# Causal attention stage: sign of the maxima on GpSimd, multiplications merged to five, masks behind a buffer's products, shift matmul moved

## The chip, the cores and the metric

One Trainium2 chip, one of its cores. The metric is the device time of one launch in microseconds. Before the change it is 1862.38 us, the median of three runs (1860.15 to 1867.64). Lower is better.

## What is computed

Two transformer layers on x of shape (4, 1024, 128) in fp32, each with a residual and a layer norm ahead of each part:

```python
x = x + _L0_attn_ref(_layernorm(x), ...)   # causal, 16 heads of 8, relative position bias
x = x + _L0_ffn_ref(_layernorm(x), ...)
x = x + _L1_attn_ref(_layernorm(x), ...)   # 16 heads
x = x + _L1_ffn_ref(_layernorm(x), ...)

# the attention that the change touches (b = 4, n = 1024, h = 16, hd = 8)
sim = jnp.einsum('bhid,bhjd->bhij', q, k)
sim = sim + jnp.transpose(bias, (2, 0, 1)) * SCALE        # bias = rel_emb[rp_bucket]
sim = sim + causal                                        # -inf where key > query
attn = jax.nn.softmax(sim, axis=-1)
out = jnp.einsum('bhij,bhjd->bhid', attn, v)
```

## The kernel before

The program runs in phases, one after the other. The change touches one of them, `attend_causal` (tag heads1). It goes through 64 pairs of head and batch; below each pair is called a head, n. All loads and stores of a head are issued by SyncE, and the engines are tied together by semaphores. Each engine works through a list written out by hand.

What happens for a head n:

- **Loads.** q and k lie in DRAM as three bf16 parts each. `load_parts` (L463) brings six pairs of parts (48 rows) into each half of the 128 partitions of qS and kS, so that a product can run in either half of the TensorE array. The loads run four heads ahead.
- **Maxima.** `maxima(n, i)` computes the scores of whole query blocks into one of two PSUM buffers psM of 1024 columns (two banks). A buffer holds one block or two: `MAXIMA = [(7,), (0, 6), (1, 5), (2, 4), (3,)]`. Bank 0 is written from the array's half of partitions 0 to 63, bank 1 from the other. The products are at L684. Behind a block's last product come two mask matmuls (`mask`, L662) that lower what lies above the diagonal. VectorE takes the maximum of each block (L582), eight reductions a head, and then writes the negated maxima as two bf16 parts: L592 (high) and L594 (the rest), which raises `nm_ready`. In TensorE's list the maxima of head n+2 are spread over head n.
- **Shift rows.** `rows(n + 1)` (L698) transposes the 16 rows of negated maxima with one matmul of 128 columns. It waits for `nm_ready`. ScalarE copies the result to mrow (L631), and SyncE writes it by two DMAs (L469) as two more rows below the q parts, so that the scores come out with the maximum already subtracted. The first scores of head n+1 wait for that.
- **Scores and exponentials.** Nine units of 512 columns (keys down, queries across, only blocks at or below the diagonal) go through a ring of three PSUM banks. The units alternate between the array's halves. TensorE writes a unit (`scores`, L712, with masks L662 on the diagonal blocks), ScalarE takes the exponential into probs (L651). The shift rows use a slot of the same ring between units 3 and 4, so `scores` of a unit waits until ScalarE has taken the unit three slots before.
- **Bias near the diagonal.** GpSimd multiplies the first 256 columns (128 for the last key block) of each key block by exp of the bias (L619), eight multiplications a head in the order `NEAR_ORDER`, each as soon as the unit named in `NEAR_AFTER` has been taken. Then it stages v of the next head (L610).
- **Values.** `values(n - 1, part)` multiplies probs and v in fp32 (L734 for both query blocks of a pair, L738 for one). A query pair c sits in its own quarter of the array's columns. The 26 entries of `VALUES` (query pair, key block) are dealt out over three parts in the list of the next head. Each matmul in fp32 is two instructions in the trace. Part 0 waits for all eight multiplications of head n-1 (`near_done`). ScalarE copies the result (L637), SyncE stores it (L473).

TensorE's list for head n, which sets the order of everything:

```python
scores(n, 0); scores(n, 1); maxima(n + 2, 0); maxima(n + 2, 1)
scores(n, 2); scores(n, 3)
values(n - 1, 0)
rows(n + 1)
scores(n, 4); maxima(n + 2, 2); scores(n, 5); scores(n, 6); maxima(n + 2, 3)
values(n - 1, 1)
scores(n, 7); scores(n, 8); maxima(n + 2, 4)
values(n - 1, 2)
```

The phase `attend_full` (heads3) does the same for the second attention, without masks, and there GpSimd already writes the two parts of the negated maxima (L871, L873) from reductions that negate (L852).

Of the kernel before, what the change touches and what calls it, by code (L numbers as in the profile page):

```python
# [18 lines left out]
ALU = mybir.AluOpType  # L19
ACT = mybir.ActivationFunctionType  # L20
AXX = mybir.AxisListType.X
# [3 lines left out]
P = 128  # L25
B = 4
# [449 lines left out]
def attend_causal(nc, m, g):  # L476
# [7 lines left out]
    ORDER = [0, 1, 2, 3, ROWS, 4, 5, 6, 7, 8]  # L484
    MAXIMA = [(7,), (0, 6), (1, 5), (2, 4), (3,)]
    NM = len(MAXIMA)
    NEAR_ORDER = [0, 1, 7, 2, 6, 3, 5, 4]
    NEAR_AFTER = [0, 2, 3, 4, 5, 6, 7, 8]
    VALUES = [[(0, 0), (1, 0), (2, 0), (3, 0), (0, 1), (1, 1), (2, 1), (3, 1), (0, 2), (1, 2), (2, 3), (3, 4), (0, 3)],
              [(0, 4), (1, 3), (2, 2), (3, 2), (0, 5), (1, 4)],  # L490
              [(0, 6), (1, 5), (2, 4), (3, 3), (0, 7), (1, 6), (2, 5)]]

    ENDS = VALUES[2][-4:]

    def place(kb, qb):

# [8 lines left out]
    def near_width(kb):  # L505
        return min(NEAR, T - kb * P)
# [24 lines left out]
    with nc.Block() as block:  # L531
# [36 lines left out]
        @block.vector  # L568
        def _(dve):
            for u in range(BUFS):  # L570
                dve.memset(kS[u][:, :], 1.0).then_inc(cleared, 1)
            for n in range(NG):
                p = n % 2
                for i, blocks in enumerate(MAXIMA):
                    dve.wait_ge(maxima_done, n * NM + i + 1)
                    at = 0
                    for qb in blocks:
                        if i == 0 and n >= 2:

                            dve.wait_ge(nm_ready, n - 1)  # L580
                        w = (qb + 1) * P
                        last = dve.tensor_reduce(mx[:, p, qb:qb + 1], psM[(n * NM + i) % 2][:, at:at + w], AXX, ALU.max)  # L582
                        if qb != blocks[-1]:
                            last.then_inc(block_taken, 1)
                        at += w
                    last.then_inc(max_taken, 1)
                dve.wait_ge(max_taken, (n + 1) * NM)
                dve.wait_ge(block_taken, (n + 1) * (TPB - NM))
                if n >= 2:

                    dve.wait_ge(slot_done, ring.rows(n - 2) + 1)
                dve.tensor_scalar(nm[:, p, 0, :], mx[:, p, :], -1.0, None, ALU.mult).then_inc(nm_hi, 1)  # L592
                dve.wait_ge(nm_hi, n + 1)
                dve.scalar_tensor_tensor(nm[:, p, 1, :], mx[:, p, :], -1.0, nm[:, p, 0, :], ALU.mult, ALU.subtract).then_inc(nm_ready, 1)  # L594

        @block.gpsimd
        def _(pool):
# [7 lines left out]
            def stage_v(n):  # L605
# [3 lines left out]
                src = g["v_all"][:, :, :, :].rearrange("p h (b t) e -> p (h b) t e", b=B)[:, n, :, :]  # L609
                pool.tensor_copy(v_ones[n % 3][:, :, 0:HD], src).then_inc(v_staged, 1)  # L610

            stage_v(0)
            for n in range(NG):
                pr = probs[n % 2]
                for kb, unit in zip(NEAR_ORDER, NEAR_AFTER):
                    pool.wait_ge(slot_taken, ring.index(n, unit) + 1)
                    a, w = place(kb, kb), near_width(kb)
                    eb = g["ebias"][:, n // B, :]
                    pool.tensor_tensor(pr[:, a:a + w], pr[:, a:a + w], bass.AP(eb.tensor, eb.offset + NEAR - 1, [list(eb.ap[0]), [-1, w]]),  # L619
                                       ALU.mult).then_inc(near_done, 1)  # L620
                if n + 1 < NG:
                    stage_v(n + 1)

# [34 lines left out]
        def _(pe):  # L658
# [6 lines left out]
            def maxima(n, i):  # L665

                if n >= NG:
                    return
                u, k = n % BUFS, n * NM + i
                if k >= 2:  # L670

                    pe.wait_ge(max_taken, k - 1)
                if i == 0:
                    pe.wait_ge(s_loaded[u], (n // BUFS + 1) * 64)
                ps = psM[k % 2]
                at = 0
                for qb in MAXIMA[i]:
                    w = (qb + 1) * P
                    for bank in range(2):
                        a, z = max(at, bank * CH), min(at + w, (bank + 1) * CH)  # L680
                        if a >= z:
                            continue
                        r, ends = HALF * bank, z == at + w
                        last = pe.matmul(ps[:, a:z], qS[u][r:r + PROWS, qb * P:(qb + 1) * P], kS[u][r:r + PROWS, a - at:z - at], start=True, stop=not ends)  # L684
                        if ends:
                            last = mask(ps[:, z - P:z], r, 1)
                    at += w
                last.then_inc(maxima_done, 1)

            def rows(n):  # L690
# [28 lines left out]
            def values(n, part):  # L719
# [2 lines left out]
                    return  # L722
                if part == 0:
                    pe.wait_ge(v_staged, n + 1)
                    pe.wait_ge(near_done, (n + 1) * TPB)
                    if n > 0:
                        pe.wait_ge(o_taken, n)
                pr, v = probs[n % 2][:, :], v_ones[n % 3]
                for c, kb in VALUES[part]:
                    out = psO[c * VW:(c + 1) * VW, 0:2 * P]  # L730
# [17 lines left out]
            for n in range(NG):  # L748
# [3 lines left out]
                maxima(n + 2, 1)  # L752
                scores(n, 2)
                scores(n, 3)
                values(n - 1, 0)
                rows(n + 1)
                scores(n, 4)
                maxima(n + 2, 2)
                scores(n, 5)
# [1245 lines left out]
```

## Time and profile before

| | us |
|---|---|
| median of three runs | 1862.38 |
| lowest, highest | 1860.15, 1867.64 |
| the profiled execution's own time | 1864.79 |
| its span, first to last instruction | 1863.1 |
| mean granted TensorE clock | 0.933 of 2.4 GHz |

Busy time of the engines over the whole span, and the same in 40 slices of 46.6 us (each digit is a tenth; the stage of the change fills slices 3 to 10 and most of the 11th):

```profile
PE 1636.9 (88%) x19058; PEld 1045.2 (56%) x19082; DVE 1517.5 (81%) x2250; ACT 1255.1 (67%) x2481; POOL 773.8 (42%) x1489
PE   5499999999745999999999639999999999999835
...
DVE  7599999999444999988555769999999999999354
```

PE is TensorE's matmuls, PEld its weight loads, DVE is VectorE, ACT ScalarE, POOL GpSimd, SP SyncE. A row of the groups below reads: line, engine, operation, output and inputs, shapes, count, then busy time and mean duration, then the idle time of the engine before them and what ended it. A row of the timeline reads: start, length, engine, line, operation; several instructions of one form that follow or overlap each other are drawn together with their count, and the bracket is the idle time before them. The ends of matmuls are modelled, their starts are recorded.

### The profile page before, as it was taken

To read this page: it belongs to the slowest core of one execution; us is meant where nothing else is said; L and a number is where in the kernel's file an instruction comes from. 1 tells how busy PE (TensorE), PEld (TensorE's weight loads), DVE (VectorE), ACT (ScalarE), POOL (GpSimd) and SP (SyncE) were. 2 spreads that over 40 slices of the span, in tenths; PEclk is the share of its full clock that TensorE was granted. 3 is DMA by queue.
4 is the path that set the end of the run, shared out by engine and by line. 5 is a ranking of instruction groups with operands and counts; after the bars stand their busy time and mean duration, and the time that the engine had idled before them with its cause. 6 is when DMAs were issued, how large, how long until landed. Compare 5 with 4: busy or idle time off the path is not lost. (4 is left out here: it accounts for less than half of the span.)

```text
span 1863.1 us, 48171 instructions
## 1 busy us (share of the span) xinstructions
PE 1636.9 (88%) x19058; PEld 1045.2 (56%) x19082; DVE 1517.5 (81%) x2250; ACT 1255.1 (67%) x2481; POOL 773.8 (42%) x1489
## 2 busy tenths in 40 slices
PE   5499999999745999999999639999999999999835
PEld 3266766776544887877677413444444444444424
DVE  7599999999444999988555769999999999999354
ACT  7378888888623444454333627988988988988734
POOL 4388888888635001000000123444444444444345
PEclk9599999999865999999999867999999999999967
DMA  8422222222171755573000351111111111111041
GB/s 270 161 77 87 86 84 87 86 85 84 44 157 26 103 93 89 94 90 59 1 1 0 122 188 40 56 58 53 55 59 54 54 59 54 54 59 48 20 102 46
DMA packets 132965, 141.87 MB, mean 76 GB/s; under 512 B 22989, under 2 KB 106122, under 8 KB 132746
## 3 DMA queue, kind: packets, MB, share of 16 engines
q1 hardware_dynamic: 132314, 138.79, 29.3%
q8 instruction: 148, 2.42, 0.5%
q14 instruction: 71, 0.58, 0.1%
q10 hardware_dynamic: 432, 0.07, 0.0%
HBM read 92.70 MB, written 44.98 MB: 74 GB/s over the span
## 5 line engine op out<-in xcount | busy, mean ns | idle before, releaser
L852 DVE TENSOR_REDUCE heads_mx<-heads_psM 128x1 f32<-128x1024 f32 x512 | 602.3, 1220 | 37.8 <-PE heads_psM L941 21.8
L921 ACT ACTIVATE heads_probs<-heads_psS 128x512 f32<-128x512 f32 x1024 | 546.0, 601 | 76.6 <-PE heads_psS L964 70.6
L890 POOL TENSOR_TENSOR heads_masked<-heads_probs,g_tri 128x128 f32<-128x128 f32 x512 | 233.7, 456 | 359.6 <-ACT heads_probs L921 359.5
L619 POOL TENSOR_TENSOR heads_probs<-heads_probs,one_ebias 128x256 f32<-128x256 f32 (+1 forms) x512 | 341.6, 690 | 82.1 <-ACT heads_probs L651 81.6
L651 ACT ACTIVATE heads_probs<-heads_psS 128x512 f32<-128x512 f32 x576 | 316.4, 603 | 65.9 <-PE heads_psS L662 60.7
L582 DVE TENSOR_REDUCE heads_mx<-heads_psM 128x1 f32<-128x1024 f32 (+7 forms) x512 | 349.6, 750 | 10.7 <-PE heads_psM L662 9.7
L941 PE MATMUL heads_psM<-heads_kS,heads_qS 48*128 48x512 bf16 x1024 | 229.9, 394 | 27.7 <-DMA heads_kS<-k_parts 18.8
L964 PE MATMUL heads_psS<-heads_qS,heads_kS 50*128 50x512 bf16 x1024 | 237.5, 388 | 0.7 <-ACT heads_probs L921 0.3
L1486 ACT ACTIVATE trees_hid_hi<-trees_hid 128x512 fp32r<-128x512 f32 x192 | 121.7, 634 | 153.3 <-DVE trees_hid L1507 151.8
L1507 DVE SCALAR_TENSOR_TENSOR trees_hid<-trees_psH,g_b,trees_chosen 128x512 f32<-128x512 f32 x192 | 144.0, 750 | 32.5 <-DMA trees_chosen<-leaf_choice 14.7
L684 PE MATMUL heads_psM<-heads_kS,heads_qS 48*128 48x512 bf16 (+3 forms) x768 | 147.8, 335 | 22.1 <-DMA heads_kS<-k_parts 19.2
L989 PE MATMUL heads_psO<-heads_probs,heads_ones_only 128*32 128x128 f32 x1920 | 161.8, 283 | 0.0
L990 PE MATMUL heads_psO<-heads_probs,heads_v_ones 128*32 128x128 f32 x1920 | 155.7, 273 | 0.0
L734 PE MATMUL heads_psO<-heads_probs,heads_v_ones 128*32 128x256 f32 x1280 | 150.9, 396 | 2.3 <-POOL heads_probs L619 2.0
L983 PE MATMUL heads_psO<-heads_probs,heads_ones_only 128*32 128x256 f32 x1280 | 148.7, 390 | 0.0
L712 PE MATMUL heads_psS<-heads_qS,heads_kS 50*128 50x512 bf16 (+3 forms) x768 | 141.4, 334 | 7.3 <-DMA heads_qS<-heads_mrow 5.4
L738 PE MATMUL heads_psO<-heads_probs,heads_v_ones 128*32 128x128 f32 x2048 | 136.6, 279 | 0.0
L1514 DVE SCALAR_TENSOR_TENSOR trees_hid_lo<-trees_hid,trees_hid_hi 128x512 fp32r<-128x512 f32 x192 | 134.2, 699 | 0.1
L964 PEld LDWEIGHTS heads_psS<-heads_qS,heads_kS 50*128 50x128 bf16 x1024 | 69.5, 93 | 114.3 <-ACT heads_probs L921 55.0
L1600 POOL COPY wide_qs<-two_qkT 128x1024 f32 (+1 forms) x4 | 4.2, 1039 | 282.6 <-SPq L1544 179.6
L983 PE MATMUL heads_psO<-heads_probs,heads_v_ones 128*32 128x256 f32 x768 | 120.9, 394 | 0.0
L989 PEld LDWEIGHTS heads_psO<-heads_probs,heads_ones_only 128*32 128x32 f32 x1920 | 72.5, 108 | 81.9 <-issue 81.8
(248 smaller groups left out, 3125.0 us busy)
## 6 DMA issues: line engine op xcount, KB each, us to landing
heads_qS<-q_parts SPq DMA_DIRECT2D x256, 96.0 KB
heads_kS<-k_parts SPq DMA_DIRECT2D x256, 96.0 KB
trees_chosen<-leaf_choice SPq DMA_DIRECT2D x96, 256.0 KB
head_outputs<-heads_oT SPq DMA_DIRECT2D x128, 128.0 KB
heads_qS<-heads_mrow SPq DMA_DIRECT2D x256, 4.0 KB
q_parts<-open_parts SPq DMA_DIRECT2D x8, 384.0 KB, 3.7
k_parts<-open_parts SPq DMA_DIRECT2D x8, 384.0 KB, 4.9
q_parts<-proj_parts SPq DMA_DIRECT2D x8, 384.0 KB, 3.3
```

Source lines behind the costliest of these rows:

```text
L582: last = dve.tensor_reduce(mx[:, p, qb:qb + 1], psM[(n * NM + i) % 2][:, at:at + w], AXX, ALU.max)
L619: pool.tensor_tensor(pr[:, a:a + w], pr[:, a:a + w], bass.AP(eb.tensor, eb.offset + NEAR - 1, [list(eb.ap[0]), [-1, w]]), ALU.mult).then_i ...
L651: act.activation(probs[n % 2][:, slot * CH:(slot + 1) * CH], ring.bank(i)[:, :], ACT.Exp).then_inc(slot_taken, 1)
L734: last = pe.matmul(out.rearrange("p (q w) -> p q w", w=P), v[:, kb, :], bass.AP(pr.tensor, a, [list(pr.ap[0]), [far - a, 2], [1, P]]), sta ...
L852: dve.tensor_reduce(mx[:, n % 2, k:k + 1], psM[k % 2][:, :], AXX, ALU.max, negate=True).then_inc(max_taken, 1)
L890: pool.tensor_tensor(masked[n % 2][:, kb, :], probs[n % 2][:, kb, kb * P:(kb + 1) * P], g["tri"][:, 0:P], ALU.mult).then_inc(near_done, 1)
L921: act.activation(probs[n % 2][:, kb, h * CH:(h + 1) * CH], ring.bank(i)[:, :], ACT.Exp).then_inc(slot_taken, 1)
L941: last = pe.matmul(psM[k % 2][:, h * CH:(h + 1) * CH], qS[u][r:r + PROWS, k * P:(k + 1) * P], kS[u][r:r + PROWS, h * CH:(h + 1) * CH], sta ...
L964: pe.matmul(ring.bank(i)[:, :], kS[u][r:r + RROWS, kb * P:(kb + 1) * P], qS[u][r:r + RROWS, h * CH:(h + 1) * CH], start=True, stop=True).t ...
L983: pe.matmul(out.rearrange("p (q w) -> p q w", w=P), v_ones[v][:, kb, :] if kb < c else ones_only[:, :], both, start=kb == 0, stop=False, t ...
L989: pe.matmul(out[:, 0:P], ones_only[:, :], pr[:, c, :], start=False, stop=False, tile_position=(0, c * VW))
L990: pe.matmul(out[:, P:2 * P], v_ones[v][:, kb, :], pr[:, b, :], start=False, stop=False, tile_position=(0, c * VW))
```

## The change

- **VectorE** no longer writes the negated maxima. Its reductions negate their result.
- **GpSimd** writes them (`minus_maxima`): a copy to bf16 and a subtraction, for head n+1, ahead of the multiplications of head n and behind the staging of v.
- **The multiplications** become five: key blocks (0, 1) after unit 2, 7 after unit 3, 6 after unit 5, (2, 3) after unit 6, (5, 4) after unit 8. A pair is one instruction over two blocks of 256 columns.
- **Values** are dealt out as 9, 10 and 7 entries instead of 13, 6 and 7. Part 0 waits for four of the five multiplications of its head, part 1 for all.
- **Maxima**: the products of a buffer alternate between its two banks, and all masks of the buffer come behind them.
- **The shift matmul** `rows(n + 1)` comes ahead of `values(n - 1, 0)` instead of behind it.

```diff
-    NEAR_ORDER = [0, 1, 7, 2, 6, 3, 5, 4]
-    NEAR_AFTER = [0, 2, 3, 4, 5, 6, 7, 8]
-    VALUES = [[(0, 0), (1, 0), (2, 0), (3, 0), (0, 1), (1, 1), (2, 1), (3, 1), (0, 2), (1, 2), (2, 3), (3, 4), (0, 3)],
-              [(0, 4), (1, 3), (2, 2), (3, 2), (0, 5), (1, 4)],
-              [(0, 6), (1, 5), (2, 4), (3, 3), (0, 7), (1, 6), (2, 5)]]
+    NEARS = [((0, 1), 2), ((7,), 3), ((6,), 5), ((2, 3), 6), ((5, 4), 8)]
+    NEAR_FIRST = 4
+    VALUES = [[(0, 0), (1, 0), (2, 0), (3, 0), (0, 1), (1, 1), (2, 1), (3, 1), (0, 2)],
+              [(1, 2), (2, 2), (3, 2), (0, 3), (1, 3), (2, 3), (3, 4), (0, 4), (1, 4), (0, 5)],
+              [(2, 4), (3, 3), (0, 6), (1, 5), (2, 5), (0, 7), (1, 6)]]
...
-                        last = dve.tensor_reduce(mx[:, p, qb:qb + 1], psM[(n * NM + i) % 2][:, at:at + w], AXX, ALU.max)
+                        last = dve.tensor_reduce(mx[:, p, qb:qb + 1], psM[(n * NM + i) % 2][:, at:at + w], AXX, ALU.max, negate=True)
...
-                dve.tensor_scalar(nm[:, p, 0, :], mx[:, p, :], -1.0, None, ALU.mult).then_inc(nm_hi, 1)
-                dve.wait_ge(nm_hi, n + 1)
-                dve.scalar_tensor_tensor(nm[:, p, 1, :], mx[:, p, :], -1.0, nm[:, p, 0, :], ALU.mult, ALU.subtract).then_inc(nm_ready, 1)
...
+            def minus_maxima(n):
+
+                p = n % 2
+                pool.wait_ge(max_taken, (n + 1) * NM)
+                pool.wait_ge(block_taken, (n + 1) * (TPB - NM))
+                if n >= 2:
+                    pool.wait_ge(slot_done, ring.rows(n - 2) + 1)
+                pool.tensor_copy(nm[:, p, 0, :], mx[:, p, :]).then_inc(nm_hi, 1)
+                pool.wait_ge(nm_hi, n + 1)
+                pool.tensor_tensor(nm[:, p, 1, :], mx[:, p, :], nm[:, p, 0, :], ALU.subtract).then_inc(nm_ready, 1)
+
+            def weight(n, blocks):
+
+                pr, eb, w = probs[n % 2][:, :], g["ebias"][:, n // B, :], near_width(blocks[0])
+                a = place(blocks[0], blocks[0])
+                step = place(blocks[-1], blocks[-1]) - a
+                at = bass.AP(pr.tensor, a, [list(pr.ap[0]), [step, len(blocks)], [1, w]])
+                by = bass.AP(eb.tensor, eb.offset + NEAR - 1, [list(eb.ap[0]), [0, len(blocks)], [-1, w]])
+                pool.tensor_tensor(at, at, by, ALU.mult).then_inc(near_done, 1)
+
             stage_v(0)
+            minus_maxima(0)
             for n in range(NG):
-                pr = probs[n % 2]
-                for kb, unit in zip(NEAR_ORDER, NEAR_AFTER):
+                if n + 1 < NG:
+                    minus_maxima(n + 1)
+                for blocks, unit in NEARS:
                     pool.wait_ge(slot_taken, ring.index(n, unit) + 1)
-                    a, w = place(kb, kb), near_width(kb)
-                    eb = g["ebias"][:, n // B, :]
-                    pool.tensor_tensor(pr[:, a:a + w], pr[:, a:a + w], bass.AP(eb.tensor, eb.offset + NEAR - 1, [list(eb.ap[0]), [-1, w]]),
-                                       ALU.mult).then_inc(near_done, 1)
+                    weight(n, blocks)
                 if n + 1 < NG:
                     stage_v(n + 1)
...
+                for j in range(max(len(of) for of in runs)):
+                    for bank in range(2):
+                        if j < len(runs[bank]):
+                            qb, a, z, first = runs[bank][j]
+                            r = HALF * bank
+                            pe.matmul(ps[:, a:z], qS[u][r:r + PROWS, qb * P:(qb + 1) * P], kS[u][r:r + PROWS, first:first + z - a],
+                                      start=j == 0, stop=j + 1 == len(runs[bank]) and (bank + 1) * CH not in [-(-e // CH) * CH for e in ends])
+                for s in range(2):
+                    for z in ends:
+                        r = HALF * ((z - 1) // CH)
+                        later = [e for e in ends if z < e <= -(-z // CH) * CH]
+                        last = pe.matmul(ps[:, z - P:z], g["masks"][r:r + HALF, s, 0, :], g["masks"][r:r + HALF, s, 1, :], start=False,
+                                         stop=s == 1 and not later)
...
-                    pe.wait_ge(near_done, (n + 1) * TPB)
+                    pe.wait_ge(near_done, n * len(NEARS) + NEAR_FIRST)
                     if n > 0:
                         pe.wait_ge(o_taken, n)
+                if part == 1:
+                    pe.wait_ge(near_done, (n + 1) * len(NEARS))
...
                 scores(n, 3)
+                rows(n + 1)
                 values(n - 1, 0)
-                rows(n + 1)
                 scores(n, 4)
```

## Rows read from the trace of the kernel before

**Rows 1.** Busy time by stretch: us, engines (instructions), clock, DMA.

```profile
100.00:440.00 340.00, 334.69 (x5783) 237.55 (x5780) 331.30 (x531) 284.95 (x583) 290.90 (x478) 1.00 0.28 86
```

**Rows 2.** Groups by shape, GpSimd's multiplications, 100 to 440 us.

```profile
L619 POOL TENSOR_TENSOR heads_probs<-heads_probs,one_ebias 128x256 f32<-128x256 f32 x372 | 261.8, 724 | 49.1 <-ACT heads_probs L651 48.6
L619 POOL TENSOR_TENSOR heads_probs<-heads_probs,one_ebias 128x128 f32<-128x128 f32 x53 | 23.9, 451 | 0.0
```

**Rows 3.** Timeline of VectorE over one head: start, length.

```profile
260.62 0.70 DVE L592 TENSOR_SCALAR heads_nm<-heads_mx 128x8 bf16<-128x8 f32 x1
261.35 0.17 DVE L594 SCALAR_TENSOR_TENSOR heads_nm<-heads_mx,heads_nm 128x8 bf16<-128x8 f32 x1
261.44 5.42 DVE L582 TENSOR_REDUCE heads_mx<-heads_psM 128x1 f32<-128x1024 f32 x8
266.90 0.69 DVE L592 TENSOR_SCALAR heads_nm<-heads_mx 128x8 bf16<-128x8 f32 x1
```

**Rows 4.** Line L592 over the whole span: duration minimum/median/maximum in ns.

```profile
L592 DVE TENSOR_SCALAR heads_nm<-heads_mx x64: 171/694/707, 78.4 to 484.9; 128x8 bf16<-128x8 f32 x64
```

**Rows 5.** Timeline of GpSimd over the same head.

```profile
258.51 2.78 POOL L619 TENSOR_TENSOR heads_probs<-heads_probs,one_ebias 128x256 f32<-128x256 f32 x4
261.24 0.23 POOL L610 COPY heads_v_ones<-one_v_all 128x64 f32<-128x64 f32 x1
261.43 0.73 POOL L619 TENSOR_TENSOR heads_probs<-heads_probs,one_ebias 128x256 f32<-128x256 f32 x1
...
264.09 3.47 POOL L619 TENSOR_TENSOR heads_probs<-heads_probs,one_ebias 128x256 f32<-128x256 f32 x5 [0.49 <-ACT heads_probs L651]
```

**Rows 6.** Timeline of TensorE's matmuls where one head ends.

```profile
266.06 0.29 PE L738 MATMUL heads_psO<-heads_probs,heads_v_ones 128*32 128x128 f32 x3
266.32 0.40 PE L712 MATMUL heads_psS<-heads_qS,heads_kS 50*128 50x512 bf16 x2
```

**Rows 7.** Waits, 100 to 440 us: total us, times, longest.

```profile
PEld heads_psS L712 <- ACT heads_probs L651: 19.7, 106, 0.2
PEld heads_psS L712 <- DMA heads_qS<-heads_mrow: 13.9, 35, 1.0
```

**Rows 8.** Groups by shape, the third stage's reductions, 1100 to 1780 us.

```profile
L852 DVE TENSOR_REDUCE heads_mx<-heads_psM 128x1 f32<-128x1024 f32 x512 | 602.3, 1220 | 37.8 <-PE heads_psM L941 21.8
```

**Rows 9.** Timeline of GpSimd in the third stage: the sign pair.

```profile
1304.82 0.19 POOL L871 CAST heads_nm<-heads_mx 128x8 bf16<-128x8 f32 x1
1305.09 0.20 POOL L873 TENSOR_TENSOR heads_nm<-heads_mx,heads_nm 128x8 bf16<-128x8 f32 x1
```

**Rows 10.** Timeline of ScalarE: units 7 and 8, units 4 to 6, units 7 and 8.

```profile
259.19 1.08 ACT L651 ACTIVATE heads_probs<-heads_psS 128x512 f32<-128x512 f32 x2 [0.29 <-PE heads_psS L662]
...
263.42 1.77 ACT L651 ACTIVATE heads_probs<-heads_psS 128x512 f32<-128x512 f32 x3 [0.16 <-PE heads_psS L662]
265.47 1.08 ACT L651 ACTIVATE heads_probs<-heads_psS 128x512 f32<-128x512 f32 x2 [0.29 <-PE heads_psS L662]
```

**Rows 11.** Timeline of TensorE: values part 0, shift matmul, scores of unit 4.

```profile
261.62 0.64 PE L734 MATMUL heads_psO<-heads_probs,heads_v_ones 128*32 128x256 f32 x8
...
262.40 0.51 PE L738 MATMUL heads_psO<-heads_probs,heads_v_ones 128*32 128x128 f32 x9
262.73 0.22 PE L698 MATMUL heads_psS<-g_identb,heads_nm 128*16 128x128 bf16 x1
262.88 0.39 PE L712 MATMUL heads_psS<-heads_qS,heads_kS 50*128 50x512 bf16 x1
```

**Rows 12.** Timeline of TensorE: maxima of blocks (2, 4), values part 1, scores.

```profile
263.92 0.40 PE L684 MATMUL heads_psM<-heads_kS,heads_qS 48*128 48x384 bf16 x2
264.09 0.29 PE L662 MATMUL heads_psM<-g_masks 64*128 64x128 bf16 x3
...
264.36 0.30 PE L738 MATMUL heads_psO<-heads_probs,heads_v_ones 128*32 128x128 f32 x2
...
264.93 0.40 PE L712 MATMUL heads_psS<-heads_qS,heads_kS 50*128 50x128 bf16 x3
```

More of the change, by code:

```diff
@@ L486, in attend_causal @@
     NM = len(MAXIMA)
-    NEAR_ORDER = [0, 1, 7, 2, 6, 3, 5, 4]
-    NEAR_AFTER = [0, 2, 3, 4, 5, 6, 7, 8]
-    VALUES = [[(0, 0), (1, 0), (2, 0), (3, 0), (0, 1), (1, 1), (2, 1), (3, 1), (0, 2), (1, 2), (2, 3), (3, 4), (0, 3)],
-              [(0, 4), (1, 3), (2, 2), (3, 2), (0, 5), (1, 4)],
-              [(0, 6), (1, 5), (2, 4), (3, 3), (0, 7), (1, 6), (2, 5)]]
-    ENDS = VALUES[2][-4:]
+    NEARS = [((0, 1), 2), ((7,), 3), ((6,), 5), ((2, 3), 6), ((5, 4), 8)]
[3 more added lines that the diff above has]
+              [(2, 4), (3, 3), (0, 6), (1, 5), (2, 5), (0, 7), (1, 6)]]
+    ENDS = [(3, 3), (2, 5), (0, 7), (1, 6)]
     def place(kb, qb):
@@ L586, in _ @@
                     last.then_inc(max_taken, 1)
[L587 to L591, printed above, removed]
-                dve.tensor_scalar(nm[:, p, 0, :], mx[:, p, :], -1.0, None, ALU.mult).then_inc(nm_hi, 1)
-                dve.wait_ge(nm_hi, n + 1)
-                dve.scalar_tensor_tensor(nm[:, p, 1, :], mx[:, p, :], -1.0, nm[:, p, 0, :], ALU.mult, ALU.subtract).then_inc(nm_ready, 1)
         @block.gpsimd
@@ L675, in maxima @@
                 ps = psM[k % 2]
-                at = 0
+                runs, ends, at = ([], []), [], 0
                 for qb in MAXIMA[i]:
@@ L680, in maxima @@
                         a, z = max(at, bank * CH), min(at + w, (bank + 1) * CH)
[L681 to L686, printed above, removed]
-                    at += w
+                        if a < z:
+                            runs[bank].append((qb, a, z, a - at))
+                    at += w
+                    ends.append(at)
+                for j in range(max(len(of) for of in runs)):
[11 more added lines that the diff above has]
+                                         stop=s == 1 and not later)
                 last.then_inc(maxima_done, 1)
```

## The prediction

> **What bounds the kernel now.** I read the busy time by stage first. The diff touches only the causal attention stage, so every other stage should stay as it is. Between 100 and 440 us, all inside that stage, the clock is at its full level (2.4 GHz), and TensorE (335 of 340 us) and VectorE (331 of 340) both look full [rows 1]. Instructions that come once a head stand there 53 times [rows 2], so a head takes 340 / 53 = 6.415 us.
>
> Two engines are seldom both the limit, so next I looked at what fills VectorE's head. Its eight reductions run without a gap, 5.42 us. Then comes L592, 8 elements in 0.70 us, and L594, 8 elements in 0.17 us [rows 3]. An operation on 8 elements doesn't need 0.7 us: over the 64 heads L592's minimum is 171 ns, its median 694 [rows 4]. GpSimd's line gives the reason: L592 starts at 260.62 and ends at 261.32, and GpSimd's multiplication beside it is the last of four that end at 258.51 + 2.78 = 261.29 [rows 3, 5]. So L592 waits for GpSimd. About 0.5 us of each head is a wait that is booked as VectorE's work; its own is near 5.42 + 0.17 + 0.17 and gaps, 5.8 us. It is not the limit.
>
> TensorE is. A smooth head takes 266.90 - 260.62 = 6.28 us [rows 3], and at its end the values products (until 266.06 + 0.29 = 266.35) and the next head's first scores (266.32) follow without idle time [rows 6]. Its waits in the stretch are two: unit 3's scores for the exponential of unit 0 (19.7 us over 106 waits), and in some heads the first scores for the DMA of the shift rows (13.9 us over 35 waits, up to 1.0) [rows 7]. The second makes most of the difference between 6.28 and the mean of 6.415.
>
> **The change, part by part.**
>
> *VectorE loses L592 and L594*, 0.70 + 0.17 us of its line. Since it isn't the limit, I book nothing. Reductions with the sign inside cost the same: the third stage has them at 1220 ns for 1024 elements [rows 8], and the 4608 elements of a head's eight take 5.42 us here, 1.20 for 1024 [rows 3].
>
> *GpSimd gains the sign pair.* The third stage has the same pair: L871 starts at 1304.82, L873 0.27 us later and lasts 0.20 [rows 9].
>
> *Eight multiplications become five* over the same elements. 128 elements take 451 ns, 256 take 724: 273 ns for each further 128, about 178 fixed [rows 2]. Back to back the 256-wide ones follow each other every (3.47 - 0.72) / 4 = 0.69 us [rows 5]. A 512-wide one is in no row; worked out, it holds GpSimd for 0.69 + 2 x 0.273 = 1.23 us. Bounds: above 1.37, two single ones; below 1.0, if the two-block pattern hid more than one start. I take 1.23. Three merges save about 3 x 0.14 = 0.4 us a head of an engine with idle time: nothing booked. But the last group, blocks 5 and 4, is now one piece of 1.23 us that can only start when unit 8's exponential is done; today block 5 is multiplied before that.
>
> *The shift matmul (L698) moves ahead of the first values part.* This step decides. It waits for nm_ready, and behind it in TensorE's order stand values part 0 and the scores of unit 4, so ScalarE's exponentials from unit 4 on wait too, and SyncE's issue of the shift rows and of the loads behind it hangs on the copy of its result. When is nm ready? GpSimd's order is: last group of head n-1, staging of v, sign pair of head n+1, groups of head n. Counted from the end of unit 8's exponential, 259.19 + 1.08 = 260.27 [rows 10]:
> - to GpSimd's start 0.07 to 0.08 (the exponential of unit 4 ends at 263.42 + 0.60 = 264.02, GpSimd starts at 264.09 [rows 5, 10])
> - last group 1.23
> - staging of v to the next instruction 0.19 (261.24 to 261.43 [rows 5])
> - sign pair 0.27 + 0.20 [rows 9]
> - to TensorE 0.07, taken from the hand-over above.
>
> That is 2.04 us, so L698 starts at 260.27 + 2.04 = 262.31. TensorE is ready for it where values part 0 starts today, at 261.62 [rows 11]. So TensorE stands still for 0.69 us in every head. Today nm is ready at 261.35 + 0.17 = 261.52 [rows 3], L698 comes at 262.73, and nothing is lost.
>
> What is late next follows round the loop. *From L698 to values part 0*: 0.05 if nothing drains between them (bounds 0 and 0.15). Today L698 starts 0.18 us before the modelled end of the values ahead of it (262.40 + 0.51 = 262.91), while the scores behind it start 0.15 after it, though it streams only 128 columns [rows 11]. I read that as no drain between values and L698, and one before scores. The Trainium skill, "TensorEngine Tiling (Array Packing)", Key Properties, says that changing the tiling mode drains TensorE and another tile of the same mode doesn't. If by that page L698 is a mode of its own, a head costs 0.1 us more, 6 us in all; the row speaks for the mode of the values. *Values part 0*: today's part 1 has 256 columns for each quarter of the array and takes 264.36 to 264.93 = 0.57 [rows 12]. Today's part 0 has 640 and takes 262.73 - 261.62 = 1.11 up to L698. The 0.10 of changing to scores apart, 128 columns cost (1.11 - 0.47) / 3 = 0.21. The new part 0 has 512: 0.57 + 2 x 0.21 = 1.00. *From unit 4's scores* (262.88) to the end of unit 8's exponential (265.47 + 1.08 = 266.55) it is 3.67 today, plus 0.21 because part 1 grows by 128 columns: 3.88 [rows 10, 11]. Round the loop: 2.04 + 0.05 + 1.00 + 3.88 = **6.97 us a head**, against 6.415.
>
> In that loop VectorE (5.42 and gaps) and GpSimd (3 x 1.23 + 0.69 + 0.41 + 0.19 + 0.47 = 5.45) have room. The shift rows' DMA gets 0.69 us more of it than in a smooth head, where its longest wait is 1.0 and most are far shorter [rows 7], so nearly all of these waits vanish; that is in the difference already, which is taken against the mean.
>
> *Maxima products alternate between the halves, masks behind them.* That gains only if a mask of one half holds back the product of the other. In block pair (2, 4) the 384-column product of one half and the 512-column product of the other start together at 263.92 (two instructions within 0.40 us), and masks start at 264.09, though two of them stand ahead of the 512-column product in the program [rows 12]. The halves already overlap: nothing booked, bounds -0.05 and +0.05 us for the two pair buffers that lie inside the loop.
>
> The sum: 61 heads in the steady state x (6.97 - 6.415) = 33.9 us. The start adds about 0.5 (head 1's L698 already waits behind head 0's last group), and the end gives back about 0.7, as values part 0 of the last head waits for four groups instead of all. So 1864.8 + 33.7 for the profiled execution, whose time is 2.4 above the median of 1862.4; against the median **1896 us**. A group of 1.37 with a drain and the buffers' 0.05 (+0.29 a head) gives 1914, a group of 1.0 with the buffers' -0.05 (-0.28 a head) 1879.
>
> **Rivals.**
> *Faster: VectorE is the limit after all.* It has no gap in a smooth head [rows 3]. If so, and if nm came in time, a head would fall to TensorE's own work, 6.28 less part of the 19.7 / 53 = 0.37 us that unit 3 waits [rows 7], about 6.1: 61 x -0.3 = -19, so 1843. It decides if nm is ready within 261.62 - 260.27 = 1.35 us of unit 8's exponential, which leaves 0.54 for the 512-wide group. A 128-wide block alone takes 0.45, and the wait inside L592 speaks against it as well.
>
> *Same: masks do hold back the other half today, or the group is much shorter.* If TensorE kept to strict order, each pair buffer inside the loop would now wait out its masks, and the change would take some 0.2 us off each of the two: 6.97 - 0.40 = 6.57, 61 x 0.155 = +9, so 1872. The pair (2, 4) row speaks against it [rows 12]. The Trainium skill, "TensorE: Matmul & The Clock Gate", Part 3, says that matmuls start strictly in program order; this trace doesn't agree, it shows the product 0.17 us ahead of earlier masks. A group of 0.85 us would give the same 1872.
>
> *Same: the change doesn't do what it says*, and the sign pair is taken ahead of the last group, so that nobody waits. The order of the loop excludes it. It would leave 6.3 to 6.415 us a head, 1856 to 1862.
>
> **How the numbers follow.** Slower by the wait of L698, 1896 (own range 1877 to 1914): 0.77. The cases near today's time, 1856 to 1872: 0.13. The faster one, 1843: 0.10. The range leaves out the faster case and part of the middle one: 1864 to 1914. A measurement of this kernel tells about 0.5%, 9 us, from no change.
>
> **What would show it.** TensorE idle for about 0.7 us before L698 in each head, put down to GpSimd; L698 2.0 us behind unit 8's exponential; GpSimd's 512-wide form at about 1.27 us; even distances of 6.97 us between heads; hardly a wait for the DMA of the shift rows; VectorE's share of the stage down from 0.97 to about 0.8 without any gain. Wrong would be: no idle time ahead of L698, a 512-wide form under 0.9 us, or a head under 6.4 us.

## The result, and the profile after

The changed kernel takes **1894.64 us** (median of four runs, 1893.71 to 1896.67) against 1862.64 for the kernel before on the same chip: a ratio of 1.0169, 95% interval 1.0148 to 1.0190. It is 32.0 us slower; 1896 was predicted, within 1864 to 1914. Its profiled execution took 1894.83, with a span of 1893.1. Below, the stretch from 100 to 440 us as in [rows 1], then GpSimd's 512-wide piece by shape as in [rows 2] (total, mean ns, idle time before them and what ended it), then the waits as in [rows 7].

```profile
100.00:440.00 340.00, 312.14 (x5343) 214.37 (x5341) 269.55 (x393) 249.73 (x540) 265.75 (x393) 1.00 0.26 79
```

```profile
L622 POOL TENSOR_TENSOR heads_probs<-heads_probs,one_ebias 128x512 f32<-128x512 f32 x148 | 188.3, 1272 | 25.9 <-ACT heads_probs L662 25.9
```

```profile
ACT heads_probs L662 <- PE heads_psS L673: 90.3, 147, 0.9
DVE heads_mx L582 <- PE heads_psM L707: 70.9, 99, 1.0
PE heads_psS L719 <- POOL heads_nm L613: 27.9, 49, 0.6
```

Once-a-head work stands here 49 times, not 53: 340 / 49 = 6.94 us a head. VectorE is down from 331 us to 270 of the 340, GpSimd from 291 to 266, and TensorE too, from 335 to 312. Nobody is full any more, which is the mark of a loop of waits. The wait that closes it is new: in every head the matmul at L719 (the shift matmul, L698 before) stands 27.9 / 49 = 0.57 us for GpSimd's pair. The waits for the shift rows' DMA, 13.9 us in [rows 7], are gone from the list.

One head of it by time. GpSimd: last group, staging of v, sign pair, next head's first two groups, and the last group of the head after:

```profile
265.76 1.27 POOL L622 TENSOR_TENSOR heads_probs<-heads_probs,one_ebias 128x512 f32<-128x512 f32 x1 [0.26 <-ACT heads_probs L662]
266.97 0.24 POOL L602 COPY heads_v_ones<-one_v_all 128x64 f32<-128x64 f32 x1
267.14 0.20 POOL L611 CAST heads_nm<-heads_mx 128x8 bf16<-128x8 f32 x1
267.42 0.20 POOL L613 TENSOR_TENSOR heads_nm<-heads_mx,heads_nm 128x8 bf16<-128x8 f32 x1
267.87 1.69 POOL L622 TENSOR_TENSOR heads_probs<-heads_probs,one_ebias 128x512 f32<-128x512 f32 x2 [0.26 <-ACT heads_probs L662]
...
272.70 1.27 POOL L622 TENSOR_TENSOR heads_probs<-heads_probs,one_ebias 128x512 f32<-128x512 f32 x1 [0.27 <-ACT heads_probs L662]
```

TensorE where the shift matmul stands:

```profile
266.83 0.27 PE L673 MATMUL heads_psS<-g_masks 64*128 64x128 bf16 x2
267.67 0.22 PE L719 MATMUL heads_psS<-g_identb,heads_nm 128*16 128x128 bf16 x1 [0.57 <-POOL heads_nm L613]
267.77 0.64 PE L757 MATMUL heads_psO<-heads_probs,heads_v_ones 128*32 128x256 f32 x8
...
268.78 0.39 PE L733 MATMUL heads_psS<-heads_qS,heads_kS 50*128 50x512 bf16 x1
```

ScalarE: units 7 and 8, unit 0, units 1 to 3, units 4 to 6, units 7 and 8, unit 0 of the next head:

```profile
264.60 1.08 ACT L662 ACTIVATE heads_probs<-heads_psS 128x512 f32<-128x512 f32 x2 [0.65 <-PE heads_psS L673]
265.95 0.60 ACT L662 ACTIVATE heads_probs<-heads_psS 128x512 f32<-128x512 f32 x1 [0.26 <-PE heads_psS L673]
...
266.70 1.58 ACT L662 ACTIVATE heads_probs<-heads_psS 128x512 f32<-128x512 f32 x3
...
269.31 1.58 ACT L662 ACTIVATE heads_probs<-heads_psS 128x512 f32<-128x512 f32 x3 [0.93 <-PE heads_psS L673]
271.54 1.09 ACT L662 ACTIVATE heads_probs<-heads_psS 128x512 f32<-128x512 f32 x2 [0.65 <-PE heads_psS L673]
272.89 0.60 ACT L662 ACTIVATE heads_probs<-heads_psS 128x512 f32<-128x512 f32 x1 [0.27 <-PE heads_psS L673]
```

The loop closes: unit 8's exponential ends at 264.60 + 1.08 = 265.68, L719 starts 1.99 later at 267.67, values part 0 0.10 later, scores 4 after another 1.01, and the next unit 8's exponential ends at 272.63, 3.85 after these. Sum 6.95. Last groups lie 272.70 - 265.76 = 6.94 apart.

Now read the same rows for something the prediction did not ask. The shift matmul writes into the ring of three banks, in slot 4, so it also waits until ScalarE has taken slot 1, unit 1. That exponential is the first of the three at 266.70 and ends near 266.70 + 0.60 = 267.30. TensorE is ready at 266.83 + 0.27 = 267.10. So two waits stand side by side, and the profile names only the one that ends last.

### The profile page after: what moved, and what is told of

It reads as the page before. It is cut to its first block and busy times, and to the rows that moved or that the text cites. A ratio compares the mean times of both kernels' runs of the same rounds, so it can differ in the third digit from the quotient of the medians.

```text
span 1893.1 us, 47979 instructions
## 1 busy us (share of the span) xinstructions
PE 1637.0 (86%) x19058; PEld 1035.6 (55%) x19082; DVE 1470.6 (78%) x2122; ACT 1238.2 (65%) x2481; POOL 770.0 (41%) x1425
## 5 line engine op out<-in xcount | busy, mean ns | idle before, releaser
L622 POOL TENSOR_TENSOR heads_probs<-heads_probs,one_ebias 128x512 f32<-128x512 f32 (+2 forms) x320 | 314.6, 1000 | 91.2 <-ACT heads_probs L662 91.1
L701 PE MATMUL heads_psM<-heads_kS,heads_qS 48*128 48x512 bf16 (+3 forms) x768 | 164.7, 332 | 22.1 <-DMA heads_kS<-k_parts 19.0
L733 PE MATMUL heads_psS<-heads_qS,heads_kS 50*128 50x512 bf16 (+3 forms) x768 | 155.9, 331 | 1.0 <-ACT heads_probs L662 0.8
L707 PE MATMUL heads_psM<-g_masks 64*128 64x128 bf16 x1024 | 125.8, 220 | 0.0
```

The costliest lines, as they stand in the source:

```text
L622: pool.tensor_tensor(at, at, by, ALU.mult).then_inc(near_done, 1)
L733: last = pe.matmul(ps[:, at:at + count], kS[u][r:r + RROWS, kb * P:(kb + 1) * P], qS[u][r:r + RROWS, first:first + count], start=True, sto ...
```

## The experiments

Kernels are compared by times since a head's first exponential, that of unit 0. In the changed kernel the shift matmul starts 267.67 - 265.95 = 1.72 after it.

**Is it the one moved line?** e1 is the changed kernel with it moved back, e2 the kernel before with it alone moved.

```diff
# e1, from the changed kernel (e2: the reverse, on the kernel before)
-                rows(n + 1)
                 values(n - 1, 0)
+                rows(n + 1)
                 scores(n, 4)
```

> The changed kernel with one part undone: the shift matmul comes behind values part 0 again. Theory (TensorE's wait for GpSimd's sign pair ahead of the shift matmul is the whole loss): the pair is ready 2.0 us behind unit 8's exponential, TensorE gets to the matmul only 1.35 + 0.90 = 2.25 us behind it, so the wait is gone and a head falls from 6.94 to between 6.28 and 6.37 us. Time 1855 to 1861 us. Rival (the new sharing out of the values, the merged multiplications or the masks behind the products cost the time): it stays between 1880 and 1895.

> The kernel before with one part of the change alone: the shift matmul ahead of values part 0, sign pair still on VectorE. Theory: VectorE has the pair ready 0.1 us before TensorE gets there, so there is no wait; time 1855 to 1862 us. Rival (the place of the matmul costs by itself, by a drain or by the exponentials behind it coming later): 1870 to 1896.

e1: 1855.39 us (1852.95 to 1858.74), inside the range of its theory; ratio to before 0.9941 (0.9924 to 0.9958). With that one line back the changed kernel is the faster one, so the line is worth 1.0169 against 0.9941, 2.3%. e2: 1888.50 (1886.55 to 1891.25), ratio 1.0124 (1.0105 to 1.0142). My theory expected e2 to be free, because VectorE's L594 is ready early enough. It is not free, and e2's TensorE, then ScalarE and VectorE beside it, say why:

```profile
271.60 0.22 PE L698 MATMUL heads_psS<-g_identb,heads_nm 128*16 128x128 bf16 x1 [0.35 <-ACT heads_probs L651]
```

```profile
270.10 0.60 ACT L651 ACTIVATE heads_probs<-heads_psS 128x512 f32<-128x512 f32 x1 [0.26 <-PE heads_psS L662]
...
270.85 1.59 ACT L651 ACTIVATE heads_probs<-heads_psS 128x512 f32<-128x512 f32 x3
```

```profile
270.90 0.17 DVE L594 SCALAR_TENSOR_TENSOR heads_nm<-heads_mx,heads_nm 128x8 bf16<-128x8 f32 x1
```

VectorE is indeed not the cause: L594 ends at 271.07, and TensorE is idle only from 271.60 - 0.35 = 271.25 on. The matmul starts 1.50 after the first exponential and 0.15 after unit 1's exponential (270.85 + 0.60 = 271.45), and the wait of 0.35 us is put down to ScalarE. That is the slot of the ring. The time lies in the range of e2's rival, that the place costs by itself; the next runs separate the two.

**Is GpSimd's order the cause, or the ring?** e3 is the changed kernel with the sign pair of head n+2 ahead of the last group, so that nm is ready long before.

```diff
             minus_maxima(0)
+            minus_maxima(1)
             for n in range(NG):
-                if n + 1 < NG:
-                    minus_maxima(n + 1)
                 for blocks, unit in NEARS:
+                    if unit == 8 and n + 2 < NG:
+                        minus_maxima(n + 2)
                     pool.wait_ge(slot_taken, ring.index(n, unit) + 1)
```

> The changed kernel with GpSimd's sign pair of head n+2 taken ahead of the last group of head n (blocks 5 and 4), instead of the pair of head n+1 behind it. Theory: the maxima are complete about when unit 8's exponential ends, the pair is ready before TensorE gets to the shift matmul, the wait of 0.69 us is gone, a head takes 6.2 to 6.35 us; time 1850 to 1861 us. Rival (GpSimd's work, not its order, holds the loop): it stays over 1885.

e3: 1883.95 us (1880.42 to 1887.63), ratio 1.0105 (1.0086 to 1.0124). The theory of the prediction, that nothing else waits once nm is in time, is wrong. In e3's code the line numbers are one higher again: L720 is the shift matmul, L663 the exponential. e3's TensorE, then its ScalarE, then its waits between 100 and 440 us:

```profile
269.73 0.22 PE L720 MATMUL heads_psS<-g_identb,heads_nm 128*16 128x128 bf16 x1 [0.35 <-ACT heads_probs L663]
269.85 0.64 PE L758 MATMUL heads_psO<-heads_probs,heads_v_ones 128*32 128x256 f32 x8
...
270.86 0.39 PE L734 MATMUL heads_psS<-heads_qS,heads_kS 50*128 50x512 bf16 x1
```

```profile
268.22 0.60 ACT L663 ACTIVATE heads_probs<-heads_psS 128x512 f32<-128x512 f32 x1 [0.26 <-PE heads_psS L674]
...
268.98 1.58 ACT L663 ACTIVATE heads_probs<-heads_psS 128x512 f32<-128x512 f32 x3
...
274.97 0.60 ACT L663 ACTIVATE heads_probs<-heads_psS 128x512 f32<-128x512 f32 x1 [0.26 <-PE heads_psS L674]
```

```profile
PE heads_psS L720 <- ACT heads_probs L663: 17.9, 51, 0.4
```

A head takes 274.97 - 268.22 = 6.75 us. GpSimd is no longer named; L720 stands 17.9 / 51 = 0.35 us for unit 1's exponential (it ends at 269.58, L720 starts at 269.73, 1.51 after the first exponential). So the late pair costs 6.94 - 6.75 = 0.19 us a head; the rest is there without it.

The rest can be split with e1, where values part 0 comes first. Its TensorE, then unit 0's exponential on ScalarE in three heads in a row:

```profile
271.99 0.64 PE L757 MATMUL heads_psO<-heads_probs,heads_v_ones 128*32 128x256 f32 x8
...
272.88 0.22 PE L719 MATMUL heads_psS<-g_identb,heads_nm 128*16 128x128 bf16 x1
```

```profile
270.90 0.60 ACT L662 ACTIVATE heads_probs<-heads_psS 128x512 f32<-128x512 f32 x1 [0.31 <-PE heads_psS L673]
...
277.14 0.60 ACT L662 ACTIVATE heads_probs<-heads_psS 128x512 f32<-128x512 f32 x1 [0.27 <-PE heads_psS L673]
...
283.39 0.60 ACT L662 ACTIVATE heads_probs<-heads_psS 128x512 f32<-128x512 f32 x1 [0.27 <-PE heads_psS L673]
```

e1's head is 283.39 - 277.14 = 6.25, a little under the 6.28 to 6.37 expected. Its values start 271.99 - 270.90 = 1.09 after the first exponential. From there it takes 0.89 to the shift matmul and 0.15 more to scores 4, as before [rows 11]. e3 takes 0.12 from the shift matmul to values and 1.01 from there. Thus e3's scores 4 come (1.51 - 1.09) + (1.13 - 1.04) = 0.42 + 0.09 = 0.51 later: 0.42 is the wait for the ring, 0.09 the order of the two. That is the 6.75 - 6.25 = 0.50 of its head. (The expectation of e9 below puts the bank's release 0.05 behind unit 1's exponential; the rows of e2 and e3 show 0.15 from that end to the start of the matmul.)

**Does the length of GpSimd's chain set the head, in the changed kernel?** e6 puts a memset of 256 columns between the staging of v and the sign pair; e5 does block 5 after unit 7 and block 4 after unit 8 as before, so only 256 columns are left behind unit 8.

```diff
# e6
                     stage_v(n + 1)
+                    pool.memset(spare[:, :], 0.0)
# e5
-    NEARS = [((0, 1), 2), ((7,), 3), ((6,), 5), ((2, 3), 6), ((5, 4), 8)]
+    NEARS = [((0, 1), 2), ((7,), 3), ((6,), 5), ((2, 3), 6), ((5,), 7), ((4,), 8)]
```

> The changed kernel with a memset of 256 columns on GpSimd between the staging of v and the sign pair, about 0.25 us of its time. Theory (in the changed kernel GpSimd's chain ends last, ring and TensorE earlier): every head grows by the same 0.25 us, to 7.19; 61 x 0.25 = +15, 1906 to 1914 us. Rival (another wait ends last): under 1900 us.

> The changed kernel with the last group split: block 5 after unit 7, block 4 after unit 8. Taken alone the chain behind unit 8's exponential would shrink by 0.54 us; but GpSimd is still at the group of blocks (2, 3) when unit 7 is done, so block 4 starts about 0.4 us later than it could, and the pair is only 0.14 us earlier. Below that stands the ring's wait, 0.19 us under today's head. Theory: 6.80 us a head, 1884 to 1889 us. Rival (the chain behind unit 8 is all that counts and there is no second wait): 6.40 us, 1862 us.

e6: 1911.64 us (1910.25 to 1911.87), ratio 1.0262 (1.0245 to 1.0280). Its GpSimd:

```profile
264.97 1.27 POOL L623 TENSOR_TENSOR heads_probs<-heads_probs,one_ebias 128x512 f32<-128x512 f32 x1 [0.26 <-ACT heads_probs L664]
...
266.35 0.31 POOL L635 MEMSET heads_spare<- 128x256 f32 x1
266.61 0.19 POOL L612 CAST heads_nm<-heads_mx 128x8 bf16<-128x8 f32 x1
...
272.17 1.27 POOL L623 TENSOR_TENSOR heads_probs<-heads_probs,one_ebias 128x512 f32<-128x512 f32 x1 [0.26 <-ACT heads_probs L664]
```

The memset holds GpSimd for 266.61 - 266.35 = 0.26 us and the head grows from 6.94 to 7.20, by the same 0.26. In that direction GpSimd's chain passes one to one into the head. e5: 1889.28 us (1888.59 to 1889.69), ratio 1.0133 (1.0115 to 1.0151), 0.3 us above its theory's range; head 6.78 by its shift matmuls:

```profile
265.07 0.22 PE L719 MATMUL heads_psS<-g_identb,heads_nm 128*16 128x128 bf16 x1 [0.41 <-POOL heads_nm L613]
271.85 0.22 PE L719 MATMUL heads_psS<-g_identb,heads_nm 128*16 128x128 bf16 x1 [0.41 <-POOL heads_nm L613]
```

The wait for GpSimd falls from 0.57 to 0.41 us. One 256-wide piece instead of the 512-wide takes 0.54 us off the chain (1.27 to 0.73), but GpSimd does its four last pieces in a row there and starts the last one late, so only 0.16 us reaches TensorE.

**Can the move be made free?** e9 is e3 with the shift matmul behind the first four entries of values part 0. TensorE then has work while unit 1's exponential ends. e10 does that to the kernel before, and e11 to the changed kernel with its late pair. The lines below are the main part of the edit; beside them, head 0 issues its shift matmul by itself, as it has no values ahead.

```diff
-                for c, kb in VALUES[part]:
+                for e, (c, kb) in enumerate(VALUES[part]):
+                    if part == 0 and e == 4 and shift is not None:
+                        rows(shift)
```

> The changed kernel with the sign pair early (as in the run before that did so) and the shift matmul after the first four of values part 0's nine entries, that is about 0.45 us further back, still ahead of most of them. The trace of the run with the early pair shows the matmul waiting for the ring: its PSUM bank is free only 0.05 us behind unit 1's exponential, which ends 1.36 us behind the head's first exponential, 0.3 to 0.4 us later than TensorE gets there. Theory (two waits stand at that place, GpSimd's and the ring's, and either alone holds TensorE): both are past at the new place, a head takes 6.24 us as with the matmul behind part 0, time 1853 to 1858 us. Rival (coming ahead of the values costs by itself, by drains or by later exponentials): over 1870 us.

> The kernel before with one edit: the shift matmul after the first four entries of values part 0, 0.45 us behind the place where it lost 24 us. The sign pair stays on VectorE, nothing else is changed. Theory (what the move costs is the ring: the bank of unit 1, whose exponential ends 1.36 us behind the head's first): no wait is left, a smooth head takes 6.28 us, and the copy of the rows comes 0.2 us earlier, so there are fewer waits for the shift rows' DMA; 1855 to 1862 us. Rival (the matmul among or ahead of the values costs by itself): 1870 us or more.

> The changed kernel with the one edit of moving the shift matmul after the first four entries of values part 0; the sign pair stays behind GpSimd's last group. There the ring is free (1.5 us behind the first exponential), but the pair is ready only at 1.72. Theory (the two waits stand side by side, each with its own time): 0.18 us of waiting for GpSimd is left, a head takes 6.42 us, 1860 to 1867 us. Rival (only one of the waits is real): 6.24 us and 1854, or 6.94 us and 1895.

e9: 1854.04 us (1853.17 to 1855.57), ratio 0.9956 (0.9940 to 0.9973). e10: 1856.29 (1855.89 to 1859.51), 0.9960 (0.9945 to 0.9975). e11: 1864.66 (1863.56 to 1867.30), 1.0004 (0.9994 to 1.0013). All three fall in the range that the two waits give. In e9 TensorE no longer stands still ahead of the matmul, and the values go on at once:

```profile
268.82 0.64 PE L761 MATMUL heads_psO<-heads_probs,heads_v_ones 128*32 128x256 f32 x8
269.28 0.22 PE L720 MATMUL heads_psS<-g_identb,heads_nm 128*16 128x128 bf16 x1
269.28 0.39 PE L761 MATMUL heads_psO<-heads_probs,heads_v_ones 128*32 128x256 f32 x3
```

e11's ScalarE has unit 0 at 261.30 and 267.73, 6.43 apart against e9's 6.24 (267.74 and 273.98): the late pair costs 0.19 here as it does from e3 to the changed kernel, and TensorE's weight load for L719 waits for GpSimd once a head, 25.4 us over 53 between 100 and 440.

e10 shows that the move can pay. Its smooth head is 6.28 us as before, but the shift rows leave earlier, and the waits for their DMA fall from 13.9 us over 35 [rows 7] to 7.3 over 23. That is 6.6 us less in 340, and an estimate of 6.6 x 61 x 6.415 / 340 = 7.6 us for the whole stage, against 1864.61 - 1856.29 = 8.3 measured on the same chip. e1, e9 and e10 are the fastest kernels of the study; the intervals of their ratios overlap, and I don't rank them.

**What is the order of the maxima worth?** e4 is the changed kernel with the maxima code of before.

```diff
-                runs, ends, at = ([], []), [], 0
...
+                at = 0
+                for qb in MAXIMA[i]:
...
+                        if ends:
+                            last = mask(ps[:, z - P:z], r, 1)
```

> The changed kernel with the maxima products and masks in their old order. Theory (the array's halves already ran beside each other before): no difference, 1892 to 1897 us. Rival (today's order gains a little inside the pair buffers): the old order costs 0.1 to 0.4 us a head more, 1901 to 1919 us.

e4: 1898.99 us (1897.12 to 1901.55), ratio 1.0181 (1.0163 to 1.0199). Its ScalarE:

```profile
260.98 0.60 ACT L662 ACTIVATE heads_probs<-heads_psS 128x512 f32<-128x512 f32 x1 [0.26 <-PE heads_psS L673]
...
264.35 1.77 ACT L662 ACTIVATE heads_probs<-heads_psS 128x512 f32<-128x512 f32 x3 [0.93 <-PE heads_psS L673]
266.62 1.09 ACT L662 ACTIVATE heads_probs<-heads_psS 128x512 f32<-128x512 f32 x2 [0.51 <-PE heads_psS L673]
267.97 0.60 ACT L662 ACTIVATE heads_probs<-heads_psS 128x512 f32<-128x512 f32 x1 [0.26 <-PE heads_psS L673]
```

The time lies between the ranges of the theory (no difference, up to 1897) and of the rival (from 1901). 6.99 a head against 6.94, so the new order gains 0.05 us. It is gained between units 4 and 7, where blocks (1, 5) and (2, 4) are: 266.62 - 264.35 = 2.27 against 271.54 - 269.31 = 2.23 in the changed kernel. The intervals of the two kernels overlap in time; the distance between heads tells them apart.

**Is VectorE really not the limit before?** e7 is the kernel before with a ninth reduction, of 256 elements, into a spare column.

```diff
+                        if qb == 1:
+                            dve.tensor_reduce(spare[:, :], psM[(n * NM + i) % 2][:, at:at + w], AXX, ALU.max)
                         last = dve.tensor_reduce(mx[:, p, qb:qb + 1], psM[(n * NM + i) % 2][:, at:at + w], AXX, ALU.max)
```

> The kernel before with a ninth reduction of 256 columns on VectorE in each head, 0.34 us back to back. Theory (half a microsecond of its head is the wait for GpSimd inside the sign's first instruction, and that wait shortens by as much): that instruction falls from 0.70 to about 0.4 us, and the time stays within 5 us of the kernel before. Rival (VectorE is the limit in a smooth head): +0.34 x 61 = +21 us.

e7: 1870.94 us (1868.26 to 1872.39), ratio 1.0044 (1.0030 to 1.0058). VectorE, then GpSimd beside it, then the waits:

```profile
259.60 0.42 DVE L584 TENSOR_REDUCE heads_spare<-heads_psM 128x1 f32<-128x256 f32 x1
...
263.04 0.37 DVE L595 TENSOR_SCALAR heads_nm<-heads_mx 128x8 bf16<-128x8 f32 x1
```

```profile
259.91 3.47 POOL L622 TENSOR_TENSOR heads_probs<-heads_probs,one_ebias 128x256 f32<-128x256 f32 x5 [0.49 <-ACT heads_probs L654]
```

```profile
PEld heads_psM L687 <- DVE heads_mx L585: 9.5, 52, 0.2
```

The sign instruction (L592 before) falls from 0.70 us [rows 3] to 0.37 and ends at 263.41, just behind GpSimd's piece (259.91 + 3.47 = 263.38), as its length being a wait demands. But the added 0.34 us isn't free: TensorE now waits in every head for VectorE to give back a buffer of psM, 9.5 / 52 = 0.18 us each time, a wait that L684 does not have before. The distance between heads grows by the same 0.18, from 6.28 to 6.46 (the exponentials of unit 0 start at 256.35 and 262.81). Neither number of the expectation came true: the price is 8.6 us against the 1862.36 of the same chip, above the 5 of my theory and far below the 21 of the rival. It is less than 61 x 0.18 = 11 because the waits for the shift rows' DMA shrink, from 13.9 us [rows 7] to 5.3. VectorE had slack, but only about 0.34 - 0.18 = 0.16 us of it at that place, not the 0.5 that the sign instruction's wait suggests.

**Can the ring's wait be covered by scores instead?** e8 moves values part 0 and the shift matmul between units 2 and 3.

```diff
-    ORDER = [0, 1, 2, 3, ROWS, 4, 5, 6, 7, 8]
+    ORDER = [0, 1, 2, ROWS, 3, 4, 5, 6, 7, 8]
...
                 scores(n, 2)
-                scores(n, 3)
-                rows(n + 1)
                 values(n - 1, 0)
+                rows(n + 1)
+                scores(n, 3)
                 scores(n, 4)
```

> The changed kernel with values part 0 between the scores of units 2 and 3 and the shift matmul behind it, ahead of unit 3; its slot in the ring is then between units 2 and 3. In the kernel before TensorE stands 0.2 us still ahead of unit 3, for unit 0's exponential. Theory (a head is as long as TensorE's list with its waits): part 0 covers that wait, the shift matmul is reached 1.75 to 1.85 us behind the first exponential, when GpSimd's pair (2.0 us behind unit 8's exponential) and the ring are just ready; a head takes 6.05 to 6.2 us, the DMA of the shift rows being what may hold it now; time 1838 to 1852 us. Rival (the order of the values is indifferent, or ScalarE runs dry): 1855 us or more.

e8: 1880.12 us (1879.25 to 1881.22), ratio 1.0097 (1.0080 to 1.0114). A clear miss. Its ScalarE, and the waits:

```profile
269.75 0.27 ACT L642 ACTIVATE heads_mrow<-heads_psS 16x128 bf16<-16x128 f32 x1 [0.32 <-PE heads_psS L719]
270.15 2.07 ACT L662 ACTIVATE heads_probs<-heads_psS 128x512 f32<-128x512 f32 x4
```

```profile
PEld heads_psS L733 <- ACT heads_probs L662: 28.5, 153, 0.2
```

Unit 3's exponential starts 2.57 us after the first (267.58) where the changed kernel has it at about 1.7, and unit 6 needs its slot. ScalarE has nothing to do behind unit 2 until the shift matmul is through. The weight loads of the scores wait for ScalarE three times a head, 28.5 / 51 = 0.56 us together, where e9 has 10.7 us over 54 waits, 0.20 a head. That is most of the difference of their heads (6.67 and 6.24); which of the three waits sets it was not separated. A bank of its own for the shift rows would take them out of the ring; it wasn't tried, since no bank was free.

## Why the prediction came out as it did

The terms of the loop, predicted and measured in the changed kernel:

| step | predicted | measured |
|---|---|---|
| unit 8's exponential to the shift matmul | 2.04 | 1.99 |
| of it the 512-wide group, to the next start | 1.23 | 1.21 |
| TensorE idle ahead of it | 0.69 | 0.57 |
| to values part 0 | 0.05 | 0.10 |
| values part 0 | 1.00 | 1.01 |
| scores 4 to the end of unit 8's exponential | 3.88 | 3.85 |
| a head | 6.97 | 6.94 |

The 512-wide group lasts 1.27 as a single instruction, but the staging of v starts 266.97 - 265.76 = 1.21 behind its start, and that is what the sum needs. The head grew by 6.94 - 6.415 = 0.525 us, times 61 heads 32.0, which is the difference of the medians.

**Right:** that the moved matmul decides and waits for GpSimd, the length of the 512-wide group inside its bounds, the price of the larger values part, that the DMA waits vanish, and that VectorE's share falls (to 269.6 / 340 = 0.79) without a gain. That three merged multiplications save nothing by themselves was not tested.

**Wrong, though the sum doesn't show it:** the step "TensorE is ready for it where values part 0 starts today", followed by GpSimd as the only thing waited for. The shift matmul is also the fifth slot of a ring of three, a wait that the code of `rows` states, and it never entered the sum. By e2 and e3 it ends at 1.51 us after the first exponential, so with nm in time the move still costs 0.42 us of waiting. Only the last 0.2 of the 0.6 us belongs to GpSimd alone. The total was right because the later of two parallel waits was the one summed, and that it was the later one had not been checked: that part is luck. Two statements built on it fall: the rival in which "nobody waits" at 6.3 to 6.415 a head (e3 measured 6.75), and the 1.35 us by which nm would have to be ready for the faster case.

**Mis-sized:** the step from the shift matmul to values, taken as 0.05, is 0.10 (0.12 in e3), inside the bounds given. The maxima order, booked at nothing with bounds of 0.05, gains 0.05 a head (e4), the whole bound; the reason given against a gain, the overlap in [rows 12], is true of the pair shown, but some time was left in it. The rival of strict order would have given 0.2 for each buffer, and that is refuted. VectorE was called far from the limit: for this change that held, yet e7 shows that 0.34 us more costs about half of it (0.18 a smooth head).

**Not asked:** the other parts together gain. With the line back e1 is at 0.9941, 9.4 us under the 1864.84 of its chip. Some 61 x (6.28 - 6.25) = 2 us of them are the smooth head, where the maxima order gains; another 3 go with less waiting for the shift rows' DMA (e1's list has 11.0 us over 37 waits against 13.9 over 35 in [rows 7], so 2.9 less in 340 us). These two make about 5 of the 6 us by which e1's profiled execution (1858.74) lies under that of before (1864.79); the remainder of the 9.4 was not traced, nor why e1 waits less for the DMA. That the smooth head gains by the order of the maxima is taken from e4, not tested in e1.

## What to carry to other kernels

Before an instruction is moved up, list every semaphore it waits for, its output buffer's release among them, and put a time to each: the profile names only the last to end, and removing that one gives only the distance to the next (0.19 us here, of the 6.94 - 6.25 = 0.69 that the line costs a head). If an instruction must be early, put it behind a few instructions of the work that needs nothing, not ahead of all of it: e9 and e10 have the same matmul only 0.46 us behind the start of the values, and neither loses anything by it. And a small operation that usually lasts four times its minimum may hold a wait (0.694 against 0.171 us here, and e7 shortened it); but the slack it seems to show isn't all there.

## What was not expected of the hardware

A bf16 matmul with 16 output rows amid the fp32 values costs next to nothing (e9: it starts at 269.28, and so do the values behind it; from the start of the values to scores 4 it is 269.87 - 268.82 = 1.05 us, against 1.01 in the changed kernel without it), while ahead of them it takes 0.10 to 0.13 us until they start (changed kernel, e3, e2) and 0.15 until scores start behind it. The Trainium skill, "TensorEngine Tiling (Array Packing)", Key Properties, says that a change of tiling mode drains TensorE; e9 shows no such drain between this matmul and the values around it. The 0.10 ahead of them therefore seems to have another reason, which no run here separates.

An instruction of VectorE on 8 elements ended 0.03 us behind GpSimd's piece whether it began 0.67 or 0.34 us before that piece's end ([rows 3, 5] and e7). The one behind it, L594, with two inputs from SBUF, ran beside the staging of v and took 166 to 169 ns in all 64 heads, without such a wait. The Trainium skill, "GPSIMD Engine Reference", 1. Specifications, says that GpSimd's SBUF interfaces are shared with VectorE, with contention for VectorE's two-port modes or two SBUF inputs. The first of the two instructions would agree if it ran in a two-port mode, which no row shows; the second has two SBUF inputs and shows no contention beside the staging of v.
